# A state-space scan: the decayed state kept in PSUM, and the inputs of a pair prepared ahead of its exponential

## What is computed

```python
def step(h, inp):                       # h: batch 8 x 512 channels x 16 states
    u_t, dt_t, B_t, C_t = inp
    dA = jnp.exp(jnp.clip(dt_t[..., None] * A, -20.0, 0.0))
    dB_u = jnp.clip(dt_t[..., None] * B_t[:, None, :] * u_t[..., None], -10.0, 10.0)
    h = jnp.clip(h * dA + dB_u, -100.0, 100.0)
    y = jnp.einsum('bds,bs->bd', h, C_t)
    return (h, y)
_, ys = jax.lax.scan(step, h0, xs)      # 1024 steps in time, one after another
```

## Time and profile before

| | us |
|---|---|
| median of 3 runs | 6645.08 |
| lowest and highest | 6643.51, 6648.44 |
| time of the profiled execution | 6640.38 |
| its span, first to last instruction | 6638.7 |
| DVE's scan instructions, first to last start | 4413.3 to 5977.8 |
| one turn of the scan | 24.42 |

### The profile page before, as it was taken

The page is one execution under the profiler, slowest core; times in us unless marked ns, Lnnn a source line. Parts: engine busy times, 40 slices in busy tenths (PEclk is TensorE's granted clock), DMA queues, the critical chain, the costliest instruction groups (busy, mean ns, idle before and its releaser), DMA issues. The chain is left out here.

```text
span 6638.7 us, 95330 instructions
## 1 busy us (share of the span) xinstructions
PE 5016.2 (76%) x27420; PEld 2058.7 (31%) x27420; DVE 4896.9 (74%) x9319; ACT 3869.7 (58%) x6353; POOL 1429.3 (22%) x1658
## 2 busy tenths in 40 slices
PE   6979799797979799795999644426666666667778
PEld 3333333333333333333666322201111111114555
DVE  6666564756666564755888688979999999996768
ACT  5555555555555555553444466667777777774443
POOL 0000000000000000000111244444433434434421
PEclk8989899898989999897999866655555555558999
DMA  0000000000000000001111233331111111114432
GB/s 23 1 13 1 14 1 1 14 1 14 1 14 1 14 1 1 7 1 36 41 41 43 64 116 115 113 97 43 42 44 44 42 43 42 44 40 151 154 98 70
DMA packets 198908, 273.62 MB, mean 41 GB/s; under 512 B 13989, under 2 KB 157989, under 8 KB 192454
## 3 DMA queue, kind: packets, MB, share of 16 engines
q1 hardware_dynamic: 181190, 252.90, 12.6%
q10 hardware_dynamic: 17408, 16.78, 0.7%
HBM read 151.14 MB, written 118.49 MB: 41 GB/s over the span
## 5 line engine op out<-in xcount | busy, mean ns | idle before, releaser
L643 DVE TENSOR_REDUCE at_nmax<-at_ps_s 128x1 f32<-128x1024 f32 x1024 | 1248.9, 1224 | 640.7 <-PE at_ps_s L342 639.4
L485 ACT ACTIVATE at_probsT<-at_ps_t 128x512 f32<-128x512 f32 x2048 | 1111.5, 594 | 831.5 <-PE at_ps_t L367 831.4
L1928 PE MATMUL sc_da<-sc_parts,sc_sel 24*128 24x512 bf16 x1024 | 527.0, 616 | 596.8 <-DVE sc_decayed L2017 507.1
L2027 DVE CUSTOM_DVE_ANT_0 sc_state<-sc_xd,sc_decayed 128x256 f32<-128x256 f32 x2048 | 787.6, 426 | 137.8 <-POOL sc_xd L1902 137.8
L1902 POOL TENSOR_SCALAR sc_xd<-sc_xd 128x1024 f32<-128x1024 f32 x512 | 584.4, 1141 | 942.5 <-ACT sc_xd L1987 942.5
L1981 ACT ACTIVATE sc_da<-sc_da,sc_a_col 128x1024 f32<-128x1024 f32 x512 | 557.1, 1088 | 375.4 <-PE sc_da L1928 375.3
L2017 DVE SCALAR_TENSOR_TENSOR sc_decayed<-sc_da,sc_state 128x256 f32<-128x256 f32 x2048 | 766.3, 416 | 6.4 <-ACT sc_da L1981 6.4
L363 PE MATMUL at_ps_t<-at_qkT 108*128 108x512 bf16 x2048 | 663.9, 385 | 64.9 <-ACT at_probsT L485 35.5
L342 PE MATMUL at_ps_s<-at_qkT 108*128 108x512 bf16 x2048 | 666.5, 410 | 26.3 <-DVE at_nmax L643 12.1
L1987 ACT ACTIVATE sc_xd<-sc_ps_du,sc_bt 128x512 f32<-128x512 f32 x1024 | 644.4, 684 | 0.0
L376 PE MATMUL at_ps_o<-at_probsT,at_v 128*32 128x256 f32 x8192 | 628.3, 390 | 1.4 <-ACT at_probsT L485 1.4
(11 more groups left out here) (307 smaller groups left out, 8059.1 us busy)
## 6 DMA issues: line engine op xcount, KB each, us to landing
dt_parts<-si_pt SPq DMA_DIRECT2D x64, 384.0 KB, 2.6
du_parts<-si_pu SPq DMA_DIRECT2D x64, 384.0 KB, 3.2
sc_parts<-dt_parts SPq DMA_DIRECT2D x128, 192.0 KB
sc_parts<-du_parts SPq DMA_DIRECT2D x128, 192.0 KB
u_tok<-si_ut SPq DMA_DIRECT2D x8, 2048.0 KB, 8.3
y<-sc_yo SPq DMA_DIRECT2D x256, 64.0 KB
so_yin<-y SPq DMA_DIRECT2D x32, 512.0 KB
so_uin<-u_tok SPq DMA_DIRECT2D x32, 512.0 KB
```

The lines of the kernel that those rows point to most:

```text
L485: nc.scalar.activation(probsT[:, c % RING, u * HALF:(u + 1) * HALF], ps_t[u][:], ACT.Exp).then_inc(s_exp, 1)
L643: nc.vector.tensor_reduce(nmax[:, par, t:t + 1], ps_s[t % 2][:], AX_X, ALU.max, negate=True).then_inc(s_max, 1)
L1928: dt_done = nc.tensor.matmul(da[q % 2][:, j], sel[0:KR, :], parts[0:KR, h, q % HP * 2 + j], start=True, stop=True)
L2027: nc.vector._custom_dve(bass.dve_ops.TENSOR_ADD_SAT, out=state[:, j % SRING, ch], in0=xd[:, q % RING, j % 2, ch], in1=decayed[:, ch], s0=S ...
```

## The change

`decayed` moves from SBUF to a PSUM bank. To free that bank, the two tiles `ps_y` become one, so the first `add_y` of a turn must wait until ACT has stored the turn before. The dt and du matmuls of a pair become two functions: in turn q PE issues first both dt matmuls of pair q+2, then both du matmuls of pair q+3. `add_y` is issued one place later: at even q, with the last round of a turn at q = 0 of the next. ACT takes the inputs of pair n+1 right behind the exponential of pair n, ahead of the exponential of pair n+1, and stores y after pair q = 1 instead of q = 3.

```diff
-        decayed = sb("decayed", [ROWS, DI])
...
-        ps_y = [psum(f"ps_y{g}", [P, HALF]) for g in range(2)]
+        ps_y = psum("ps_y", [P, HALF])
+        decayed = psum("decayed", [ROWS, DI])
...
-            def replicate(it, q, first=False):
+            def replicate_dt(it, q, first=False):
                 n = it * NPAIR + q
                 h = q // HP
                 if q % HP == 0:
-                    for c in range(2):
-                        pe.wait_ge(s_in[h][c], 16 * it + 16)
+                    pe.wait_ge(s_in[h][0], 16 * it + 16)
                 if not first:
                     pe.wait_ge(s_dec, (n - 1) * 2 * NC)
                 for j in range(2):
-                    bank = slice(j * HALF, (j + 1) * HALF)
-                    dt_done = nc.tensor.matmul(da[q % 2][:, j], sel[0:KR, :], parts[0:KR, h, q % HP * 2 + j],
-                                               start=True, stop=True)
-                    if j == 1:
-                        dt_done.then_inc(s_rdt, 1)
+                    last = nc.tensor.matmul(da[q % 2][:, j], sel[0:KR, :], parts[0:KR, h, q % HP * 2 + j],
+                                            start=True, stop=True)
+                last.then_inc(s_rdt, 1)
+
+            def replicate_du(it, q, first=False):
+                n = it * NPAIR + q
+                h = q // HP
+                if q % HP == 0:
+                    pe.wait_ge(s_in[h][1], 16 * it + 16)
+                for j in range(2):
                     if not (first and q == 0):
                         pe.wait_ge(s_xd, 2 * n - 1 + j)
-                    du_done = nc.tensor.matmul(ps_du[:, bank], sel[Q1:Q1 + KR, :],
-                                               parts[Q1:Q1 + KR, h, q % HP * 2 + j], start=True, stop=True)
-                du_done.then_inc(s_rdu, 1)
+                    last = nc.tensor.matmul(ps_du[:, j * HALF:(j + 1) * HALF], sel[Q1:Q1 + KR, :],
+                                            parts[Q1:Q1 + KR, h, q % HP * 2 + j], start=True, stop=True)
+                last.then_inc(s_rdu, 1)
 
             def add_y(it, g, r):
                 if r == 0:
                     pe.wait_ge(s_cw, it + 1)
-                    if not (isinstance(it, int) and it < 2):
-                        pe.wait_ge(s_yo, it - 1)
+                    pe.wait_ge(s_yo, it)
...
             def turn(it, g, first, last):
                 for q in range(NPAIR):
                     if q + LEAD < NPAIR:
-                        replicate(it, q + LEAD)
+                        replicate_dt(it, q + LEAD)
                     elif not last:
-                        replicate(it + 1, q + LEAD - NPAIR)
-                    if q % 2 == 1:
-                        add_y(it, g, q // 2)
+                        replicate_dt(it + 1, q + LEAD - NPAIR)
+                    if q + LEAD + 1 < NPAIR:
+                        replicate_du(it, q + LEAD + 1)
+                    elif not last:
+                        replicate_du(it + 1, q + LEAD + 1 - NPAIR)
+                    if q % 2 == 0 and q > 0:
+                        add_y(it, g, q // 2 - 1)
+                    elif q == 0 and not first:
+                        add_y(it - 1, 1 - g, ROUNDS - 1)
...
             def turn(it, g, first, last):
                 for q in range(NPAIR):
                     n = it * NPAIR + q
-                    act.wait_ge(s_rdt, n + 1)
-                    flat = da[q % 2][:].rearrange("p j d -> p (j d)")
-                    nc.scalar.activation(flat, flat, ACT.Exp, scale=a_col[:]).then_inc(s_da, 1)
-                    act.wait_ge(s_rdu, n + 1)
-                    if not first or q >= RING:
-                        act.wait_ge(s_state, (n - RING + 1) * 2 * NC)
-                    for j in range(2):
-
-                        nc.scalar.activation(xd[:, q % RING, j], ps_du[:, j * HALF:(j + 1) * HALF], ACT.Copy,
-                                             scale=bt[:, bass.ds(2 * n + j, 1)]).then_inc(s_xd, 1)
-                    if q == HP - 1 and not first:
+                    decays(n, q)
+                    if not (last and q == NPAIR - 1):
+                        inputs(n + 1, q + 1, first and q + 1 < RING)
+                    if q == 1 and not first:
                         store(it - 1, 1 - g)
 
+            inputs(0, 0, True)
             schedule(act, turn)
```

More of the change, by code:

```diff
@@ L1945, in add_y @@
                     c0 = (r * STRIPS + s) * VW
-                    last = nc.tensor.matmul(ps_y[g][s * VW:(s + 1) * VW, :], cw[g][:, c0:c0 + VW],
+                    last = nc.tensor.matmul(ps_y[s * VW:(s + 1) * VW, :], cw[g][:, c0:c0 + VW],
                                             state[:, (r * STRIPS + s) % SRING], start=(r == 0), stop=(r == ROUNDS - 1))
@@ L1952, in turn @@
                     if q + LEAD < NPAIR:
-                        replicate(it, q + LEAD)
+                        replicate_dt(it, q + LEAD)
                     elif not last:
-                        replicate(it + 1, q + LEAD - NPAIR)
-                    if q % 2 == 1:
-                        add_y(it, g, q // 2)
+                        replicate_dt(it + 1, q + LEAD - NPAIR)
[7 more added lines that the diff above has]
+                        add_y(it - 1, 1 - g, ROUNDS - 1)
             for q in range(LEAD):
-                replicate(0, q, first=True)
+                replicate_dt(0, q, first=True)
+            for q in range(LEAD + 1):
+                replicate_du(0, q, first=True)
             schedule(pe, turn)
+            add_y(NI - 1, 1, ROUNDS - 1)
         @block.scalar
@@ L1973, in store, with decays, inputs @@
                     act.wait_ge(s_st[g], (it - g) * 8 * STRIPS)
-                nc.scalar.copy(yo[:, g], ps_y[g][:]).then_inc(s_yo, 1)
+                nc.scalar.copy(yo[:, g], ps_y[:]).then_inc(s_yo, 1)
+            def decays(n, q):
+                act.wait_ge(s_rdt, n + 1)
+                flat = da[q % 2][:].rearrange("p j d -> p (j d)")
+                nc.scalar.activation(flat, flat, ACT.Exp, scale=a_col[:]).then_inc(s_da, 1)
+            def inputs(n, q, fresh=False):
+                act.wait_ge(s_rdu, n + 1)
+                if not fresh:
+                    act.wait_ge(s_state, (n - RING + 1) * 2 * NC)
+                for j in range(2):
+                    nc.scalar.activation(xd[:, q % RING, j], ps_du[:, j * HALF:(j + 1) * HALF], ACT.Copy,
+                                         scale=bt[:, bass.ds(2 * n + j, 1)]).then_inc(s_xd, 1)
             def turn(it, g, first, last):
```

## The result

The changed kernel takes 6680.72 us (median of 4 runs, 6680.5 to 6688.21), the kernel before 6645.44 beside it. The ratio is 1.0055, 95% interval 1.0038 to 1.0073: slower by 35 us, or 0.55%. The forecast was 6673, slower by 0.4%. The profiled execution took 6680.78, its span is 6679.1.

A forecast was written before the change was run, and what follows sets the result against it. A ring through PE, DVE, ACT and POOL's clip was taken to bound the kernel. The new chain and store gave 24.90 us a turn against 24.42, 29 us more: 6673 us, 0.4% slower, range 6630 to 6720.

The forecast's parts named there:

- The new ring: Chain from exp of one odd pair to the next through inputs, du, add_y and dt: 5.80 us for two pairs.
- this part: Inputs taken a pair ahead: two pairs go from 6.05 to 5.80 us, a gain of 1.2 us a turn.
- The change of shape on the way back: PE going from add_y to the next dt: 0.14 us. Rival, free or hidden by a weight load: 6637 us, chance 0.09.
- The store: ACT's store after q = 1 waits 2.6 us for the last add_y, costing 1.70 us a turn, 63 times.
- DVE writing PSUM: DVE's decayed and state instructions with the product in PSUM: 0.335 us each, bounds 0.335 and 0.40.
- The rival with PSUM slowing DVE: Every PSUM write or read at 0.40 us: 6790 us; only decayed slower: 6689; chance 0.12 together.
- The clock: PE's granted clock stays 0.50; rival that it rises, at 2.4 GHz: 6503 us, chance 0.05.
- the one in which DVE runs without a gap: Rival: add_y and dt overlap, or ACT's wait for the store falls away: 6454 us, chance 0.03.
- The sum: A scan turn takes 4 x 5.80 + 1.70 = 24.90 us instead of 24.42: 29 us more in all.
- the spare time that the ring leaves DVE: DVE has 0.44 us to spare in two pairs, hiding instructions of up to 0.362 us on average.
- dt and du apart: PE issuing dt, dt, du, du mostly loses their overlap: some 0.9 us for two pairs, off the chain.
- its collision in the old order: DVE's state instructions, with a second SBUF input, meet POOL's weights of C once a turn: 0.2 us a turn.

The follow-up runs named there:

- Experiments 6: Changed kernel with add_y on 256 of its 512 columns, half of y not computed: 6502.72 us, ratio 0.979 to the kernel before.
- Experiment 7: Changed kernel with half of y left out and ACT's store after q = 2: 6447.99 us, ratio 0.9696 to the kernel before.
- experiment 2: Changed kernel with add_y ahead of the du matmuls in PE's queue, store still after q = 1: 6602.79 us, ratio 0.9928 to the kernel before.
- experiment 1: Changed kernel with ACT's store of y after q = 2 instead of q = 1: 6569.7 us, ratio 0.9885 to the kernel before.
- experiment 4: Changed kernel with decayed back in SBUF, one ps_y, order and store as changed: 6883.79 us, ratio 1.0352 to the kernel before.
- experiment 5: Kernel before, PE's and ACT's orders kept, with decayed in PSUM, one ps_y and the store after q = 1: 6613.04 us, ratio 0.9946.

## Why the prediction was right

**The new ring.** The forecast had 2.32 + 0.55 + 1.86 + 1.07 = 5.80 us for two pairs; the trace has 2.33 + 0.53 + 1.86 + 1.07 = 5.79. Experiments 6 and 7 show that the length of `add_y` is part of it, experiment 2 that the order of PE's queue is. In experiment 1, where the store costs nothing, 62 turns from copy to copy average 23.17 us, four rounds of 5.79, against 24.43 before: about 1.25 less, where the forecast had 1.2 for this part.

**The change of shape on the way back.** No row of the scan had it, and it was taken from attention. It came out at 1.86, as summed. Had it been free, the round would have been 5.65. That rival falls.

**The store.** 1.70 us a turn were forecast. Moving the store away gives 1.80 back (experiment 1). The 0.10 that the forecast lacked lies in one link: from the start of `add_y` to the copy 1.94 + 0.04 = 1.98 were summed, and the trace has 2.09 (4821.55 to 4823.64). ACT waits 2.68 for it, 2.6 were forecast. Without this one stall the change is a gain, so the sign of the result hangs on it.

**DVE writing PSUM.** It was taken to cost nothing; the bounds reached to 0.40 an instruction. Experiment 7 measures 0.332 for both kinds. The length of a decayed instruction grows from 416 to 424 ns, the distance of starts doesn't. The rival with PSUM slowing DVE falls. The Trainium skill, "Perfetto Trace Analysis", section "Optimizing Scalar/DVE Operations", gives DVE twice the access time on PSUM; by that figure this kernel would have shown it, and the measurement decides against it here.

**The clock** stayed at 0.50 with PE busy for 1337 of 1607 us, so that rival falls too, and so does the one in which DVE runs without a gap: ACT found `add_y` unfinished at every store. Experiment 7 shows DVE without gaps, but only with both of its conditions made: a shorter `add_y` and a later store.

**The sum.** The scan was to grow by 29 us; it grew by 1594.0 - 1564.5 = 29.5. That it came so near is partly luck. From copy to copy, averaged over 62 turns, a turn grew from 24.43 to 24.97, 0.54 where the forecast had 0.48, because of the store's 0.10. Over 63 turns and the first one, which has no store, that makes 33; 3.5 us fewer were measured, somewhere at the ends of the scan, and stood in no term. The span grew by 40.4. The other 10.9: the scan phase began 5.8 us later, behind code that isn't touched; from there to the first decayed it took 1.8 more, since ACT now takes the inputs first; and 3.3 lie behind the scan. For the 5.8 and the 3.3 no run here tells whether the change has a part in them. The medians lie 35.3 apart where 29 were forecast, and the changed kernel's, 6680.72, is 7.7 above the forecast time.

**What was wrong within it.** DVE was to wait some 0.2 us a pair and over 1.5 at q = 2, in all 180. The total is 176, but apart from the first wait of the scan (8.0) it lies at q = 2 alone, 2.68 a turn, so the agreement of the totals is luck. In between it is the state instruction that waits: 0.39 us for `add_y`, to have a place in the state's ring, once in two pairs where it does. That wait stood in no step, and it adds nothing to the time: it is the spare time that the ring leaves DVE (0.44 us in two pairs by the forecast), taken at another place. Experiment 1 has it at nearly every second pair, and the round is still 5.79. The forecast's own turn left DVE 24.90 - 21.44 = 3.46 us to wait, not 180 / 64 = 2.8; the trace has (176.3 + 49.1 - 8.0) / 63 = 3.45. *dt and du apart* was to lose the matmuls' overlap. At odd q they don't lose it: dt and du both start at 4806.04. PE had time to spare, so it cost nothing in the sum. And the product in PSUM was counted at 0.2 us a turn. That is what it is worth by its collision in the old order; there it also shortens the clip (33 us in all), and in the new order it is worth 200 (experiment 4). The forecast's total didn't suffer, since it summed the new order with the product in PSUM.

Taken apart by the scans: the product in PSUM 33 us less than before (1564.5 to 1531.4, experiment 5), the new order with the store after q = 2 another 51 less (to 1480.9, experiment 1), the store after q = 1 113 more (to 1594.0).

## What to carry to other kernels

When a stall goes, follow the queue of each engine behind it to the next ring, and add up that ring from rows: here it was only 4% shorter than the old one. A store that waits for the last product of a queue belongs where that product is done; one place too early turned a gain of 1% into a loss. Before two edits are judged one by one, ask whether the wait that one removes was what kept the other's collision away.

## What the runs showed of the hardware

- Two SBUF inputs on DVE beside a POOL instruction that reads SBUF: a state instruction took up to 1260 ns instead of 414 (experiment 4), the clip 1.04 us alone and 1.27 beside it. The weights of C took 0.65 beside two such instructions in the kernel before and 0.41 in experiment 5. With one input in PSUM none of this is left.
- DVE instructions of 256 fp32 elements, half of them writing PSUM and the others reading it, took 0.332 us of their engine each in a row without gaps (experiment 7), though the records of those that write PSUM are 421 ns long.
- Matmuls of two row groups started at the same time (4806.04, both of 24 rows x 128 columns) although the queue holds the second dt between them: by these records du's first matmul did not wait for the second dt, which started at 4806.44. The Trainium skill, "TensorEngine Tiling (Array Packing)", section "Tiling Modes", says that tiles load and multiply independently; this row agrees.
